# One GNN and mixture-of-experts layer on one core: attention and gates in one block, the last head finished by groups of tiles, x added head by head

## The reference

```python
x = x + relu(agg + res)      # graph attention, 12 heads of 64: softmax over incoming edges of
                             # leaky_relu(a1[src] + a2[dst]), weighted sum of ft[src]; res = h @ W_res
x = x + moe(layernorm(x))    # 4 experts (768 -> 384 -> 768, gelu), each node goes to argmax(z @ Wg + bg)
x = x + gcn(gcn(layernorm(x)))
x = x + ffn(layernorm(x))
```

## Time and profile before

| | |
|---|---|
| time, median of 3 runs | 1056.06 us (1055.58 to 1057.77) |
| the profiled execution | 1055.24 us, its span 1053.4 us |
| PE, DVE, ACT busy | 93%, 58%, 27% of the span |
| granted TensorE clock, mean | 0.972 |
| the twelve heads, about | 176 to 457 us of the span |
| last head, normalisation and gates, table | 457 to 506 us |
| experts | 506 to 633 us |

### The profile page before, as it was taken

How to read it: one execution, slowest core, us unless ns; L and a number is a source line. 1 busy time by engine, 2 the same in 40 slices (tenths; PEclk the granted TensorE clock), 3 DMA queues, 4 the chain that set the end, 5 groups by cost and what they waited for, 6 DMA issues and landing times. The chain is left out here.

```text
span 1053.4 us, 15653 instructions
## 1 busy us (share of the span) xinstructions
PE 980.8 (93%) x5652; PEld 793.7 (75%) x5652; DVE 607.2 (58%) x1261; ACT 287.9 (27%) x782; POOL 60.0 (6%) x114
## 2 busy tenths in 40 slices
PE   7999998999999999958599994999999999999997
PEld 4777676999999999946366652666997557888785
DVE  8887897999999999985322225552111112232331
ACT  2444344454444554213011110221111112200100
POOL 2000000000000000012122211000000000000000
PEclk9999998999999999979699996999999999999999
DMA  6000010000000001528552236114200005000001
GB/s 156 2 1 1 5 49 1 24 26 24 24 34 37 24 24 43 127 81 283 174 177 92 89 147 197 57 44 162 71 1 1 0 1 146 1 30 30 28 3 60
DMA packets 25528, 65.26 MB, mean 62 GB/s; under 512 B 5720, under 2 KB 9572, under 8 KB 25344
## 3 DMA queue, kind: packets, MB, share of 16 engines
q1 hardware_dynamic: 22833, 54.13, 16.5%
q0 software_dynamic: 2080, 10.23, 2.9%
q10 hardware_dynamic: 559, 0.16, 0.1%
HBM read 47.74 MB, written 16.76 MB: 61 GB/s over the span
## 5 line engine op out<-in xcount | busy, mean ns | idle before, releaser
L809 PE MATMUL O<-X,masks 125*125 125x264 f32 x1200 | 279.6, 333 | 2.9 <-DVE masks L954 2.9
L806 PE MATMUL O<-X,CSR 125*125 125x132 f32 x1080 | 245.1, 227 | 0.0
L809 PEld LDWEIGHTS O<-X,masks 125*125 125x125 f32 x1200 | 222.2, 187 | 3.1 <-issue 3.1
L954 DVE SCALAR_TENSOR_TENSOR masks<-a2b,NA,CSR 125x375 fp32r<-125x375 f32 (+1 forms) x360 | 212.5, 645 | 8.3 <-PE O L809 5.9
L806 PEld LDWEIGHTS O<-X,CSR 125*125 125x125 f32 x1080 | 205.2, 190 | 0.0
L1879 DVE SCALAR_TENSOR_TENSOR UL<-pw,dinv,UH 125x768 fp32r<-125x768 f32 x20 | 20.4, 1018 | 111.4 <-ACT UH L1802 111.4
L1659 PE MATMUL pw<-W 128*125 128x384 f32 x240 | 81.6, 498 | 1.0 <-ACT W L1795 1.0
L424 PE MATMUL pc<-ohs_a,ohd 125*125 125x512 f16 x375 | 77.9, 347 | 1.6 <-DVE ohs_a L629 1.6
L1659 PE MATMUL pw<-region,xr_or_h 128*125 128x384 f32 x240 | 77.6, 486 | 0.0
L151 POOL TENSOR_TENSOR rstd<-rstd,minus_half 125x1 f32<-125x1 f32 x40 | 25.4, 636 | 843.8 <-DVEq L145 843.8
L1659 PEld LDWEIGHTS pw<-W 128*125 128x125 f32 x240 | 45.5, 193 | 32.3 <-issue 3.7
(11 more groups left out here) (237 smaller groups left out, 1384.3 us busy)
## 6 DMA issues: line engine op xcount, KB each, us to landing
a2b<-a_rows SPq DMA_DIRECT2D x12, 610.4 KB
W<-in_L_ffn_W SPq DMA_DIRECT2D x4, 1152.0 KB, 5.9
WM<-in_L_ffn_W SPq DMA_DIRECT2D x4, 1152.0 KB, 8.4
xr_or_h<-in_x SPq DMA_DIRECT2D x10, 336.0 KB
region<-in_x SPq DMA_DIRECT2D x2, 1680.0 KB
z_rows<-region SPq DMA_DIRECT2D x10, 336.0 KB
region<-y_rows SPq DMA_DIRECT2D x10, 336.0 KB
x_rows<-xr_or_h SPq DMA_DIRECT2D x10, 336.0 KB
```

What stands on the lines that cost most here:

```text
L806: nc.tensor.matmul(O[0:P, bank, d - d0, 2 * DP:4 * DP], CSR[:, s, d * P:(d + 1) * P], X[:, buf, s, 4:6, :].rearrange("p k d -> p (k d)"), ...
L809: ins = nc.tensor.matmul(O[0:P, bank, d - d0, 0:4 * DP], kept, X[:, buf, s, 0:4, :].rearrange("p k d -> p (k d)"), start=s == 0, stop=s == ...
L954: nc.vector.scalar_tensor_tensor(masks[:, s, 0:(d1 - d0) * P], a2b[:, buf, d0 * P:d1 * P], NA1[:, s, bass.ds(h, 1)], CSR[:, s, d0 * P:d1 * ...
```

## The change

Attention and gates become one block, and the layer norm follows in the branch of the heads. On DVE, `combine` gives the multiplication by `rec` to ACT (ten small multiplications, `scale_rows`), and its addition and a new one, which takes the relu and adds the head's columns of x (`XH`), stand in group 2 of the next head. `add_x` over all heads is gone. Head 11 is finished by `finish_tiles` for groups of tiles, in front of tiles 0, 4 and 7 of the normalisation. PE turns tile 0 inside head 11's last group, ahead of its step 7. SP loads x by head in pieces of 64 columns, and loads expert 0 after the fifth tile of z; experts 1 to 3 follow in the expert block. POOL's constants are made during head 11.

```diff
                 def x_columns(h):
+                    if h >= 2:
+                        sp.wait_ge(s_xa, h - 1)
+                    for lo, hi in SHARES:
+                        sp.dma_start(XH[lo:hi, h % 2, :, :],
+                                     node_tiles(a["x"])[lo:hi, :, h * DH:(h + 1) * DH]).then_inc(s_xh[h % 2], 16)
...
                     for t in range(NT):
                         sp.wait_ge(s_z3, t + 1)
...
+                    if t == NT // 2 - 1:
+                        load_expert(sp, 0)
...
                             for s in range(NT):
+                                if last and g == JOBS - 1 and s == TURN_AT:
+                                    pe.wait_ge(s_ev, JOBS * h + JOBS + 1)
+                                    turn_z(0)
...
+                    def scale_rows(h):
+                        act.wait_ge(s_rec, h + 1)
+                        for t in range(NT):
+                            ins = nc.scalar.mul(whole[:, t, 0:DH], whole[:, t, 0:DH], rec[:, t:t + 1])
+                        ins.then_inc(s_nrm, 1)
...
                         if not last:
                             products(act, h + 1, 1 - buf)
+                        if not first:
+                            scale_rows(h - 1)
                         evict(h, buf, 0)
...
                     head(H - 1, 1, last=True)
+                    copy_zt(0)
                     evict(H - 1, 1, 2)
+                    gates_of_tiles()
...
+                def normalised(finished=None):
+                    for t in range(NT):
+                        if finished:
+                            finished(t)
+                        following = prepare(t)
+                        if t:
+                            z_of(t - 1, asked_at)
+                        asked_at = following
+                    z_of(NT - 1, asked_at)
...
-                        k.mark(nc.vector.tensor_tensor(whole[:, :, 0:DH], whole[:, :, 0:DH],
-                                                       rec[:, :].unsqueeze(2).broadcast_to([P, NT, DH]), ALU.mult))
-                        yield
-                        k.wait()
+                        dve.wait_ge(s_nrm, h + 1)
                         o = XR[:, :, bass.ts(h, DH)]
                         k.mark(nc.vector.tensor_tensor(o, o, whole[:, :, 0:DH], ALU.add))
                         yield
+                        k.wait()
+                        dve.wait_ge(s_xh[buf], 16 * (h - buf) + 32)
+                        nc.vector.scalar_tensor_tensor(o, o, 0.0, XH[:, buf, :, :], ALU.max, ALU.add).then_inc(s_xa, 1)
+                        yield
+
+                    def finish_tiles(t):
...
+                        dve.wait_ge(s_ev, JOBS * (H - 1) + g + 3)
+                        dve.wait_ge(s_xa, H - 1)
+                        k(nc.vector.tensor_tensor(both[:, d, :], ev[:, d, 0, :], ev[:, d, 1, :], ALU.add))
+                        k(nc.vector.tensor_tensor(whole[:, d, :], both[:, d, 0:DP], both[:, d, DP:2 * DP], ALU.add))
+                        k(nc.vector.tensor_scalar(den[:, d], whole[:, d, DH], TINY, None, ALU.max))
+                        k(nc.vector.reciprocal(rec[:, d], den[:, d]))
+                        k(nc.vector.tensor_tensor(whole[:, d, 0:DH], whole[:, d, 0:DH],
+                                                  rec[:, d].unsqueeze(2).broadcast_to([P, w, DH]), ALU.mult))
+                        k(nc.vector.tensor_tensor(o, o, whole[:, d, 0:DH], ALU.add))
+                        dve.wait_ge(s_xh[1], 16 * H)
+                        k(nc.vector.scalar_tensor_tensor(o, o, 0.0, XH[:, 1, d, :], ALU.max, ALU.add))
...
                     head(H - 1, 1, last=True)
-                    k.wait()
-                    add_x(k, (0, H - 1))
-                    for step in combine(H - 1):
-                        pass
-                    k.wait()
-                    add_x(k, (H - 1, H))
-                    k.wait()
+                    normalised(finish_tiles)
```

More of the change, by code:

```diff
@@ L177, in program @@
         heads = ExitStack()
+        with ExitStack() as aside:
+            side = sb(aside, "side", [128, NT * 6 * DP])
         X = sb(heads, "X", [P, 2, NT, 6, DP], F32R)
@@ L745, in program, with gather, expert_of @@
         slow.close()
+        edge.close()
+        gat.close()
+        ZA = XI
+        SLOTS = 3
+        XS = region[:, 0:SLOTS * D].rearrange("p (j d) -> p j d", j=SLOTS)
+        s_xs = [sem(f"slots_in{u}") for u in range(SLOTS)]
+        def gather(j):
+            nc.gpsimd.indirect_dma_start(
+                out=XS[:, j % SLOTS, :], out_offset=None, in_=z_rows,
+                in_offset=bass.IndirectOffsetOnAxis(ap=slot_node[:, j:j + 1], axis=0)).then_inc(s_xs[j % SLOTS], 16)
+        def expert_of(eng, j):
+            return eng.value_load(eid[0:1, j:j + 1], min_val=0, max_val=NEXP - 1)
@@ new lines, in program @@
+        b1r = in_side(3740, 128, NEXP * MH)
+        ones16 = in_side(3676, 63).bitcast(F16)[:, 0:P]
+        at_slot = sb(s3, "at_slot", [P, NT, 128], F16)
+        notabove16 = sb(s3, "notabove16", [P, P], F16)
+        slot = sb(s3, "slot", [P, 128])
+        tile_no = sb(s3, "tile_no", [P, 16])
+        node = sb(s3, "node", [P, NT])
+        gate = sb(s3, "gate", [P, NT, NEXP])
+        gmax = sb(s3, "gmax", [P, NT])
+        gdeg = sb(s3, "gdeg", [P, NT])
+        OH = sb(s3, "OH", [P, NEXP, NT], F16)
@@ new lines, in program @@
+        seen = sb(s3, "seen", [P, NT])
+        upto = sb(s3, "upto", [P, NEXP, NT])
+        rank = sb(s3, "rank", [P, NEXP, NT])
+        totals = sb(s3, "totals", [P, NEXP])
+        used = sb(s3, "used", [P, NEXP, 16])
+        start = sb(s3, "start", [P, NEXP])
+        first = sb(s3, "first", [1, NEXP])
+        posf = sb(s3, "posf", [P, NT])
+        reached = sb(s3, "reached", [P, NT, 16])
+        tiles = sb(s3, "tiles", [P, NT])
+        within = sb(s3, "within", [P, NT])
+        in_tile = sb(s3, "in_tile", [P, NT, 16])
@@ new lines, in turn_gates, with gates_of_tiles @@
+                def turn_gates(t):
+                    pe.wait_ge(s_gc3, t + 1)
+                    nc.tensor.transpose(pg[0:P, NEXP * t:NEXP * (t + 1)], gT[:, t * P:(t + 1) * P],
+                                        ident[0:NEXP, 0:NEXP]).then_inc(s_gt3, 1)
+                def gates_of_tiles():
+                    pe.wait_ge(s_wg, 32)
+                    for t in range(NT):
+                        if t + 1 < NT:
+                            turn_z(t + 1)
+                        gates(t)
+                        if t:
+                            turn_gates(t - 1)
+                    turn_gates(NT - 1)
@@ L792, in quickly, with head @@
                 def quickly():
                     pe.sem_inc(s_mf, NT)
-                    def head(h, buf):
+                    def head(h, buf, last=False):
                         pe.wait_ge(s_xn, h + 1)
@@ L821, in quickly @@
                         head(2 * q + 2, 0)
-                    head(H - 1, 1)
+                    head(H - 1, 1, last=True)
+                    gates_of_tiles()
                 def slowly():
@@ L984, in head @@
                             mask(h, buf, 0, s)
-                        steps = iter(()) if first else combine(h - 1)
+                        steps = iter(()) if first else combine(h - 1, 1 - buf, last)
                         for s in range(NT):
                             mask(h, buf, 1, s)
-                            if 1 <= s <= 5:
+                            if 1 <= s <= 3:
                                 next(steps, None)
@@ L993, in head @@
                                 low_parts(dve, h + 1, 1 - buf)
+                            if 2 <= s <= 3:
+                                next(steps, None)
                     head(0, 0, first=True)
                     with dve.Fori(0, H // 2 - 1) as q:
-                        k.loop(q, 10)
+                        k.loop(q, 6)
                         head(2 * q + 1, 1)
@@ new lines, in _ @@
+                ch(nc.vector.scalar_tensor_tensor(within[:, :], tiles[:, :], -float(ST), posf[:, :], ALU.mult, ALU.add),
+                   nc.vector.tensor_tensor(node_in[:, :, :], in_tile[:, :, :],
+                                           node[:, :].unsqueeze(2).broadcast_to([P, NT, 16]), ALU.mult))
+                for n in range(2):
+                    t5 = slice(5 * n, 5 * n + 5)
+                    nc.vector.tensor_tensor(at_slot[:, t5, :], slot[:, :].unsqueeze(1).broadcast_to([P, 5, 128]),
+                                            within[:, t5].unsqueeze(2).broadcast_to([P, 5, 128]),
+                                            ALU.is_equal).then_inc(s_tab, 1)
@@ new lines, in _ @@
+                ch(nc.vector.tensor_scalar(first[:, :], start[0:1, :], float(ST), None, ALU.mult))
+                ch(nc.vector.tensor_scalar(eidf[:, 0, :], tile_no[0:1, :], first[:, 1:2], None, ALU.is_ge))
+                for n, e in enumerate(range(2, NEXP)):
```

(5 more changed lines are left out.)

508 lines of the change are left out of this document (222 added, 286 removed).

## The result

The changed kernel takes 1047.12 us (median of four runs, 1046.59 to 1047.66) beside 1055.82 us before (1054.42 to 1057.77): a ratio of 0.9922, 95% interval 0.9907 to 0.9936. That is 1047.0 forecast and 1047.1 measured, and a gain of 8.7 us where 9.1 was forecast. The profiled execution took 1046.74 us, its span 1044.9 us.

The account below looks back on a forecast made before the run. PE bounds the heads; behind them DVE bounds the beginning of the stretch and PE its end. Gates 9.1 us earlier, nothing added by heads or branch: 1056.06 - 9.1 = 1047.0 us, range 1045.0 to 1051.2.

Parts of the forecast that it names:

- Heads: Twelve attention heads: moving the multiplication to ACT adds nothing; bounds -0.82 to +0.16 us, within DVE's 0.43 us reserve.
- the rival behind it: Heads: DVE waits for ACT's scaled rows and becomes the bound; 1064.3 us at 2 us per head; chance 0.11 (slower).
- DVE behind the last mask: After the heads: finishing head 11 by groups gives tile 9's z at 480.9, 6.4 us ahead of 487.29.
- PE: Last group to gates: 2.7 us stall, lower clock, tile 9 turned at 482.9 instead of 492.09; gain taken as 9.1 us.
- the clock rival: Gates: clock low again at tile 6, 1.9 us more a tile for about two tiles, 1050.7 us; chance 0.14.
- Behind the gates: Sorting and experts: small operations fit in; expert 1's later load keeps 15 of 20.7 us of cover.
- The branch: PE's jump over the spread-scores code after the gates: counted as nothing, bounds 0 to 6.1 us worse.
- The branch rival: Jump after the gates costs about 1 to 2 us, giving 1048.5 us; chance 0.06.

Follow-up runs that it names:

- e5: Changed kernel, with ACT's ten multiplications for the previous head moved behind group 1's eviction: 1120.99 us, ratio 1.0629.
- e4: Changed kernel, with the multiplication by the inverse sums back on DVE and ACT's ten multiplications left out: 1049.64 us, ratio 0.9946.
- e3: As e2, but head 11 is finished for all ten tiles at once, when the last group is out: 1055.88 us, ratio 1.0012.
- e2: Changed kernel, with tile 0 turned behind the last group of attention instead of inside it: 1048.85 us, ratio 0.9946.
- e1: Changed kernel, without the code for widely spread scores, so nothing is jumped over: 1046.91 us, ratio 0.9927.
- e7: Changed kernel, with the two forms of attention swapped in the program, so engines jump ahead of the heads: 1051.83 us, ratio 0.9967.
- e6: Changed kernel, with all turns and gates behind the branch on PE and ACT, and DVE's small operations ahead of its jump: 1048.08 us, ratio 0.9938.
- e10: As e6, with tile 4's gates multiplied twice (12 more matmuls): 1047.29 us, ratio 0.9921.
- e11: e6 run again, unchanged: 1047.79 us, ratio 0.9933.
- e9: As e6, but with tile 0 still turned inside head 11's last group: 1047.84 us, ratio 0.9946.
- e8: The changed kernel run again, unchanged: 1048.62 us.
- e12: The changed kernel run a third time, unchanged: 1050.00 us.

## Why the prediction was right, step by step

**Heads.** Right: 23.11 us apart, no wait for ACT. Two numbers in it were off. ACT's place has 3.0 us of reserve, not 2.3, and e5 shows that the rival behind it was real. DVE's reserve was not 0.43 us: the multiplication, 0.73 us from its start to the next mask's (e4), cost 0.03 us a head, so some 0.7 us: 0.47 us of idle time, and 0.23 us by which the masks beside pauses are slower.

**DVE behind the last mask.** Right within 0.5 us: last mask over at 450.75 (450.7), z of tile 0 written at 457.6 (457.4), tile 6 at 476.0 (475.8), tile 9 at 481.1 (480.9). e3 shows that the gain in time hangs on it, and 7.3 of the 8.9 us at the last gate.

**PE.** Right: the stall 3.02 us (2.7), the clock down behind it, the last heads' product at 462.9 (463.1), tile 9 turned at 483.14 (482.9), last gate 8.94 us earlier (9.1). e2 shows the stall free. The pause of about 1 us for tile 3 that the clock rival speaks of doesn't follow from the prediction's own sum (PE at tile 3 at 465.7 + 2.37 = 468.1, its z at 466.6), and there was none.

**Behind the gates.** Right: expert 1's load is issued at 510.91 instead of 518.09, and between 500 and 640 us PE waits for no expert's weights.

**The branch.** This is the term that was mis-sized: counted as nothing, it cost 1.6 us. That is 8.94 - 7.31 in the changed kernel, 1.5 by e1 (3.70 - 2.19) and 1.64 by e7. I had priced the jump by the 0.95 us in which DVE went from `combine` through the barrier to tile 0's statistics, "over code of the same kind". But the change also puts the norm and the gates of ten tiles into the form that is jumped over. The jump then leaves idle 3.1 to 3.6 us on PE and 3.4 to 5.6 us on DVE, and PE's costs 4.04 us where it comes ahead of the heads (e7). On PE 3.22 us stand against the 1.74 of cover that I had counted, a difference of 1.5; DVE's pause was over 0.3 us too late as well (it reads the gates at 488.04, 0.47 us behind the last one, before 0.14), which PE's covers. The Trainium skill (Runtime: NRT & Kernel Launch, Instruction fetch mechanics) had the mechanism: a taken branch to code that isn't at hand must fetch it first. It named no price. e1 and e7 agree with it, the pauses go with the code and move with it; that a fetch is what fills them, no run shows. The branch rival, 1048.5, was in substance right, and had a chance of only 0.06.

**Why the total fits all the same.** 9.1 became 8.94, less 1.63 for the branch is 7.31. The expert block's first product lost 1.1 us by the clock, other waits up to the last operation gave 1.3 back (7.45), and the output's last store took 1.05 us less, none of which I had counted. These last three are of the size of the differences between executions of one kernel. And the median of before, 1056.06 in the sum, is 1055.82 in the result. That 1047.0 and 1047.1 meet so closely is luck; what was right is a gain of 9 us at the gates and the path by which it comes.

**The clock rival** (0.14) didn't happen in the three profiles of the changed kernel, but did in e1, e2 and e6, at the place that it named. It cost 1.5 us, not the 3.7 that I gave it: the clock was back up after one tile. The wait ahead of it was 2.00 us each time, not the 0.6 us of its text.

## What to carry to other kernels

Where one engine finishes all tiles and the next then starts on the first, cut the finishing into the groups in which its input becomes free: without that (e3) the 9 us were gone, and removing 7.6 us of work at the same place was worth nothing. Before a stage is put inside a branch, look at how much code it adds to the other form, and for what covers the jump on each engine that is late there, and on the engine behind it: freed of one engine's pause, the kernel was held by the other's. A stall at a place with slack costs nothing (e2); taking it out moved PE's idle time to a later place, in two of four executions (e2, e6, not e10, e11) with a lower clock there.

## What was unexpected of the hardware

A jump over code that isn't run stopped DVE for 3.4 to 5.6 us and PE for 3.1 to 3.6 us, where the engine had work right behind it. But in e6, e9, e10 and e11, where PE's jump comes right behind the matmuls of the heads, there was no pause at all. The record of PE's jump sorts the runs into two groups: 3.3 to 3.8 us in the changed kernel (e8 and e12 too), e2, e3, e4 and e5, with 4.13 us in e7, and 0.31 to 0.41 us in the kernel before, e6, e9, e10 and e11. The second group differs in two things at once: the jump comes while earlier matmuls still run, and the form that isn't run is shorter, as it doesn't hold the gates of ten tiles. No run keeps one and changes the other, so which of them makes the jump short stays open. One reading speaks for the length: DVE's jump comes behind its last work in every kernel; before, where the other form doesn't hold the norm, its sequencer branched at 463.7 and stood at the block's end at 464.2, while behind the same branch 3.4 to 5.6 us pass once the norm stands in that form.

The clock: behind PE's wait of 3.02 us in the last group it went to 1.2 GHz in the changed kernel's three profiles and in e4, e7 and e9, and stayed at 2.4 GHz in e1. After 2.00 us of wait for tile 6 it fell in three executions (e1, e2, e6), and after 1.99 us it held in one (e9); after 1.56 us and less for that tile it held in all seven, and so it did in e6 after 2.35 us of wait for tile 3. Short waits are no safe side, though: at tiles 0 and 1 PE waits 0.92 and 1.31 us in e2, 0.83 and 1.38 us in e10 and e11, with only a tile's six transposes between the two, and the clock fell there in all three. It held in e6, the same kernel as e11, behind waits of 0.84 and 1.38 us. So nearly the same waits in the same code can bring the lower clock or not from one execution to the next, and what decides between them stays open. At tile 6 it cost 1.5 us; at tile 1, where PE had time to spare, nothing in the end.
